# Layer 2's bias rows of a pair of heads placed side by side and fetched in one transfer

## The reference

```python
sim = jnp.einsum('bhid,bjd->bhij', q, k)          # 2 sequences, 16 heads, one shared k and v
sim = sim + jnp.concatenate([null_col, attn_bias], axis=-1)   # attn_bias: fside, (16, 1024, 1024)
sim = jnp.where(causal_mask, neg, sim)
sim = jnp.where(mask_p[:, None, None, :], sim, neg)
attn = jax.nn.softmax(sim, axis=-1)
out = jnp.einsum('bhij,bjd->bhid', attn, v)
```

## Time and profile before

| | |
|---|---|
| median of 3 runs | 2331.18 us (2331.05 to 2338.11) |
| the profiled execution, its own time | 2349.09 us |
| its span, first to last instruction | 2347.2 us |
| what lies around the span | 1.9 us |
| TensorE busy in the span | 85% |
| VectorE, ScalarE, GpSimd busy | 71%, 57%, 45% |
| mean granted TensorE clock | 0.928 |
| first to last `add_bias` of layer 1 / 2 / 3 | 450.5 / 480.9 / 437.6 us |

### The profile page before, as it was taken

One profiled execution on the slowest core, in us unless ns is written; L12 is line 12 of the kernel. 1 busy time (PEld: TensorE's weight loads), 2 busy tenths in 40 slices (PEclk: granted clock), 3 DMA queues, 4 the chain that ended last, 5 costly groups with the idle time before them and its releaser, 6 DMA issues. The chain is left out here.

```text
span 2347.2 us, 46857 instructions
## 1 busy us (share of the span) xinstructions
PE 2003.9 (85%) x11738; PEld 1429.2 (61%) x11738; DVE 1674.6 (71%) x4082; ACT 1338.9 (57%) x2900; POOL 1066.4 (45%) x1286
## 2 busy tenths in 40 slices
PE   5996496899999999389889999995595999999988
PEld 4885363666666667376556666665463666666657
DVE  5777766777887775558667877756665887888855
ACT  2222564677776664147557766642464777777753
POOL 1342113566765652006456666622112666666632
PEclk8998597899999999699889999998697999999999
DMA  4530246333333333386677777741246334333332
GB/s 119 157 127 17 85 170 246 113 109 108 108 109 108 108 104 113 102 299 191 205 226 229 235 233 231 231 157 34 92 171 235 100 108 123 119 118 107 115 121 87
DMA packets 222215, 338.76 MB, mean 144 GB/s; under 512 B 27446, under 2 KB 104380, under 8 KB 222044
## 3 DMA queue, kind: packets, MB, share of 16 engines
q1 hardware_dynamic: 222044, 336.86, 45.6%
HBM read 250.63 MB, written 102.91 MB: 151 GB/s over the span
## 5 line engine op out<-in xcount | busy, mean ns | idle before, releaser
L1486 POOL TENSOR_SCALAR at_row<-at_row,at_inv 128x129 f32<-128x129 f32 (+7 forms) x384 | 720.2, 1876 | 364.1 <-DVE at_inv L1647 357.3
L1694 ACT ACTIVATE at_row<-at_row,at_nmax 128x129 f32<-128x129 f32 (+7 forms) x768 | 595.3, 775 | 239.8 <-DVE at_nmax L1666 238.1
L1666 DVE CUSTOM_DVE_ANT_0 at_row<-at_s,bias,at_row 128x128 f32<-128x128 f32 (+7 forms) x768 | 618.1, 810 | 67.7 <-PE at_s L1594 39.6
L1606 PE MATMUL at_t<-ident,at_row 128*128 128x128 f32 x3456 | 549.5, 283 | 53.9 <-ACT at_pt L1687 33.9
L1606 PEld LDWEIGHTS at_t<-ident,at_row 128*128 128x128 f32 x3456 | 397.3, 143 | 259.1 <-issue 182.4
L1593 PE MATMUL at_s<-k_hh,q_hl 128*128 128x512 f32 (+3 forms) x1152 | 464.6, 403 | 48.2 <-SPq L1552 26.0
L1622 PE MATMUL at_o<-at_pt,v 128*64 128x512 f32 (+3 forms) x2304 | 443.4, 507 | 6.0 <-ACT at_pt L1687 2.5
L1501 DVE COPY at_pt<-at_t 128x128 f32<-128x128 f32 (+3 forms) x576 | 278.1, 483 | 204.6 <-PE at_t L1606 186.0
L1594 PE MATMUL at_s<-k_lp,q_h 65*128 65x512 f32 (+3 forms) x1152 | 393.7, 354 | 0.0
L1687 ACT ACTIVATE at_pt<-at_t 128x512 f32<-128x512 f32 (+2 forms) x576 | 307.3, 534 | 141.5 <-PE at_t L1606 136.3
L1593 PEld LDWEIGHTS at_s<-k_hh,q_hl 128*128 128x128 f32 x1152 | 226.5, 197 | 82.4 <-DVE at_nmax L1666 28.5
(11 more groups left out here) (225 smaller groups left out, 2813.9 us busy)
## 6 DMA issues: line engine op xcount, KB each, us to landing
q_hl<-q_dram SPq DMA_DIRECT2D x192, 256.0 KB, 4.3
bias<-bands_dram SPq DMA_DIRECT2D x64, 512.0 KB, 5.7
q_dram<-pj_qh SPq DMA_DIRECT2D x96, 256.0 KB, 2.7
q_dram<-pj_ql SPq DMA_DIRECT2D x96, 256.0 KB, 2.7
q_h<-q_dram SPq DMA_DIRECT2D x96, 256.0 KB, 5.0
o_dram<-at_o_sb SPq DMA_DIRECT2D x96, 256.0 KB, 4.5
o_in<-o_dram SPq DMA_DIRECT2D x10, 2048.0 KB, 8.5
bands_dram<-brow_dram SPq DMA_DIRECT2D x2, 8192.0 KB, 32.1
```

The costliest lines, as they stand in the source:

```text
L1486: return eng.tensor_scalar(cells, cells, inv[:, i:i + 1], None, ALU.mult)
L1606: last = eng.transpose(t_ps[m % NTR][:, c * P:(c + 1) * P], row[:, u % RING, here:here + P], t["ident"][:])
L1666: eng.tensor_tensor_reduce(out=row[:, u % RING, ZERO:ZERO + width], in0=s_ps[u % 2][:, 0:width], in1=bt[:, lo:lo + width], scale=-1.0, sca ...
L1694: eng.activation(cells, cells, ACT.Exp, scale=-1.0, bias=nmax[:, i:i + 1], accum_out=rsum[:, i:i + 1]).then_inc(s["exp"], 1)
```

## The change

Both units of a pair of heads get their bias rows in one place of twice the width, one unit's rows behind the other's in each partition. One transfer fetches the left part for both heads and one fetches both diagonal blocks, each with two runs for each partition instead of one. There are 8 semaphores for pairs instead of 16 for units, VectorE waits only ahead of the even unit, and the first seven pairs, as before the first fourteen units, are fetched in `project`.

```diff
-HEAD_SLOTS, BIAS_IN_FLIGHT, ROWS_FIRST = 4, 16, 14
+HEAD_SLOTS, PAIRS_IN_FLIGHT, PAIRS_FIRST = 4, 8, 7
...
-    widths = [((u // 2) % NT + 1) * P for u in range(4 * NT)]
+    widths = [2 * (k % NT + 1) * P for k in range(2 * NT)]
...
-        last.append(max(before + [u - BIAS_IN_FLIGHT]))
+        last.append(max(before + [k - PAIRS_IN_FLIGHT]))
...
-        if tile:
-            eng.dma_start(t["bias"][:, BIAS_AT[n]:BIAS_AT[n] + width - P],
-                          bias[one, tile * P:(tile + 1) * P, 0:width - P].rearrange("o p c -> p (o c)")).then_inc(sem, 16)
-        eng.dma_start(t["bias"][:, BIAS_AT[n] + width - P:BIAS_AT[n] + width],
-                      t["corners"][one, :, width - P:width].rearrange("o p c -> p (o c)")).then_inc(sem, 16)
+    tile = n % NT
+    width = (tile + 1) * P
+    two = bass.ds(head, 2)
+    out = t["bias"][:, PAIR_AT[n]:PAIR_AT[n] + 2 * width].rearrange("p (s c) -> p s c", s=2)
+    if tile:
+        eng.dma_start(out[:, :, 0:width - P], bias[two, tile * P:(tile + 1) * P, 0:width - P].rearrange("s p c -> p s c")
+                      ).then_inc(sem, 16)
+    eng.dma_start(out[:, :, width - P:width], t["corners"][two, :, width - P:width].rearrange("s p c -> p s c")).then_inc(sem, 16)
...
-                    place.wait(eng, "biased", BIAS_AFTER[n] + 1)
-                    p, tile, side, width = unit(n)
-                    load_bias(eng, t, bias, s[f"bias{n % NBIAS}"], n, place.turn * 2 * HP + (2 * p + side))
+                    place.wait(eng, "biased", 2 * PAIR_AFTER[n] + 2)
+                    load_bias(eng, t, bias, s[f"bias{n % NBIAS}"], n, place.turn * 2 * HP + 2 * (n // NT))
...
-                    for n in range(U):
-                        if n % GU == 0:
-                            queries(place, ready, n // GU)
-                        row_bias(place, ready, n)
+                    for n in range(U // 2):
+                        if n % (GU // 2) == 0:
+                            queries(place, ready, n // (GU // 2))
+                        pair_bias(place, ready, n)
...
-                    lo = (2 * p + side + 1) * S - width if toeplitz else BIAS_AT[u % U]
-                    if not toeplitz:
-                        turn.wait_loads(eng, f"bias{slot}", row_loads(u) * U // NBIAS, row_loads(u) * (u // NBIAS + 1))
-                    elif tile == 0:
+                    lo = (2 * p + side + 1) * S - width if toeplitz else PAIR_AT[u % U // 2] + side * width
+                    if not toeplitz and side == 0:
+                        turn.wait_loads(eng, f"bias{slot}", pair_loads(slot) * (U // 2 // NBIAS),
+                                        pair_loads(slot) * (u // 2 // NBIAS + 1))
+                    elif toeplitz and tile == 0:
```

More of the change, by code:

```diff
@@ L45, in bias_places, with pair_loads @@
     last = []
-    for u, width in enumerate(widths):
-        before = [n for n in range(u - len(widths), u)
-                  if places[n] < places[u] + width and places[u] < places[n] + widths[n]]
-        last.append(max(before + [u - BIAS_IN_FLIGHT]))
+    for k, width in enumerate(widths):
+        before = [n for n in range(k - len(widths), k)
+                  if places[n] < places[k] + width and places[k] < places[n] + widths[n]]
+        last.append(max(before + [k - PAIRS_IN_FLIGHT]))
     return places, last
-BIAS_AT, BIAS_AFTER = bias_places()
-def row_loads(n):
-    return 16 if (n // 2) % NT == 0 else 32
+PAIR_AT, PAIR_AFTER = bias_places()
+def pair_loads(k):
+    return 16 if k % NT == 0 else 32
 SERIAL = count()
@@ L966, in project @@
     LAST = N + 12
-    FIRST = HEAD_SLOTS if bias is None else ROWS_FIRST
+    FIRST = HEAD_SLOTS if bias is None else PAIRS_FIRST
     names = ["dve", "var", "std", "xn", "xtr", "xt_hi", "xt_lo", "main", "sq", "ss", "norm", "inv", "inv_t",
@@ L1051, in first_bias @@
                     for n in range(FIRST):
-                        load_bias(eng, t, bias, s["first"], n, n if bias is None else n % 2)
+                        load_bias(eng, t, bias, s["first"], n, n if bias is None else 0)
                 if bias is not None:
@@ L1070, in _ @@
                     eng.wait_ge(s[f"store{n}"], 32 * NCH * NPAIR // NST)
-                eng.wait_ge(s["first"], 96 + (16 * FIRST if bias is None else sum(row_loads(n) for n in range(FIRST))))
+                eng.wait_ge(s["first"], 96 + (16 * FIRST if bias is None else sum(pair_loads(n) for n in range(FIRST))))
             @block.tensor
@@ L1403, in load_bias @@
 def load_bias(eng, t, bias, sem, n, head):
-    one = bass.ds(head, 1)
     if bias is None:
[L1407 to L1410, removed]
-        if tile:
-            eng.dma_start(t["bias"][:, BIAS_AT[n]:BIAS_AT[n] + width - P],
-                          bias[one, tile * P:(tile + 1) * P, 0:width - P].rearrange("o p c -> p (o c)")).then_inc(sem, 16)
-        eng.dma_start(t["bias"][:, BIAS_AT[n] + width - P:BIAS_AT[n] + width],
-                      t["corners"][one, :, width - P:width].rearrange("o p c -> p (o c)")).then_inc(sem, 16)
+        eng.dma_start(t["bias"][:, n * S:(n + 1) * S], t["bands"][bass.ds(head, 1), :, :].rearrange("o p c -> p (o c)")
+                      ).then_inc(sem, 16)
+        return
+    tile = n % NT
[4 more added lines that the diff above has]
+        eng.dma_start(out[:, :, 0:width - P], bias[two, tile * P:(tile + 1) * P, 0:width - P].rearrange("s p c -> p s c")
+                      ).then_inc(sem, 16)
+    eng.dma_start(out[:, :, width - P:width], t["corners"][two, :, width - P:width].rearrange("s p c -> p s c")).then_inc(sem, 16)
 def load_outputs(eng, t, sem, c):
@@ L1438, in attend @@
     toeplitz = bias is None
-    NBIAS = HEAD_SLOTS if toeplitz else BIAS_IN_FLIGHT
-    n_bias = HP * 2 if toeplitz else U
+    NBIAS = HEAD_SLOTS if toeplitz else PAIRS_IN_FLIGHT
+    n_bias = HP * 2 if toeplitz else U // 2
     pieces, starts = [], []
@@ L1447, in attend @@
     NPC = len(pieces)
-    assert NPC % 6 == 0 and U % NBIAS == 0 and U % RING == 0 and NGRP % 2 == 0
+    assert NPC % 6 == 0 and n_bias % NBIAS == 0 and U % RING == 0 and NGRP % 2 == 0
     def first(u):
@@ L1463, in slot_loads @@
     def slot_loads(n):
-        return 16 if toeplitz else row_loads(n)
+        return 16 if toeplitz else pair_loads(n)
     def unit(u):
@@ L1528, in head_bias, with pair_bias @@
                     load_bias(eng, t, None, s[f"bias{n % NBIAS}"], n, place.turn * 2 * HP + n)
-                def row_bias(place, ready, n):
-                    if ready and n < ROWS_FIRST:
+                def pair_bias(place, ready, n):
+                    if ready and n < PAIRS_FIRST:
                         return
-                    place.wait(eng, "biased", BIAS_AFTER[n] + 1)
-                    p, tile, side, width = unit(n)
-                    load_bias(eng, t, bias, s[f"bias{n % NBIAS}"], n, place.turn * 2 * HP + (2 * p + side))
+                    place.wait(eng, "biased", 2 * PAIR_AFTER[n] + 2)
+                    load_bias(eng, t, bias, s[f"bias{n % NBIAS}"], n, place.turn * 2 * HP + 2 * (n // NT))
                 def loads(place, ready):
@@ L1552, in _ @@
                     eng.sem_inc(s[f"q{g}"], 48)
-                for n in range(HEAD_SLOTS if toeplitz else ROWS_FIRST):
+                for n in range(HEAD_SLOTS if toeplitz else PAIRS_FIRST):
                     eng.sem_inc(s[f"bias{n}"], slot_loads(n))
@@ L1658, in add_bias @@
                     turn.wait(eng, "qk", u + 1)
-                    slot = (2 * p + side if toeplitz else u) % NBIAS
-                    lo = (2 * p + side + 1) * S - width if toeplitz else BIAS_AT[u % U]
-                    if not toeplitz:
-                        turn.wait_loads(eng, f"bias{slot}", row_loads(u) * U // NBIAS, row_loads(u) * (u // NBIAS + 1))
-                    elif tile == 0:
+                    slot = (2 * p + side if toeplitz else u // 2) % NBIAS
+                    lo = (2 * p + side + 1) * S - width if toeplitz else PAIR_AT[u % U // 2] + side * width
[3 more added lines that the diff above has]
+                    elif toeplitz and tile == 0:
                         turn.wait_loads(eng, f"bias{slot}", 16, 16 * (u // U + 1))
```

## The result

The changed kernel takes 2321.4 us (median of 14 runs, 2318.38 to 2329.07), the kernel before 2335.69 us beside it (14 runs, 2331.05 to 2347.21). The ratio is 0.9937, 95% interval [0.9923, 0.9951], so the change is worth some 14.7 us (the medians are 14.3 apart). The forecast had 2314 us from 2331.18, a gain of 17.4.

The account below looks back on a forecast made before the run. SyncE's number of issues at turn starts was taken to bound layer 2's attention; -13.8 - 4 - 4 = -21.8 us profiled, four fifths of it -17.4, gave 2314 us from 2331.18, range 2299 to 2330.

Parts of the forecast that it names:

- What bounds the kernel: Layer 2's attention: some 43 us of waits caused by transfers, layer 3 the floor; turn starts limited by SyncE's issues, not bytes.
- The start of a turn, -13.8: Units 0 to 8, turns 1 to 7: fewer issues and earlier release cut 17.3 us of excess to 3.5.
- The two signs that the prediction named as fatal: Layer 2: a turn-start landing over 6 us after issue (B or D), or DMA share times stage over 351 us (D).
- The half microsecond of stall that it left: Start of each of seven turns: 0.5 us of stall left, as pair 4's margin is only 0.7 us.
- What follows, -4: Units 8 to 24: half of 8.8 us of pipeline refill and lower TensorE clock goes, between 0 and -8.8.
- VectorE's code, -4: Jumps in turns 1 and 2: both fetch again, but a shorter backlog saves 4 of 18.3 us.
- Waits added, 0: Pairs 7 and 15 in SyncE's queue: their new waits for units 7 and 23 cost nothing.
- Four fifths: Whole kernel: plain runs gain four fifths of the profiled -21.8 us, so -17.4, as they may stall less.
- B: Turn starts: data come no earlier because two-run issues take SyncE longer; 2324 to 2331 us, say 2327; chance 0.17.
- D: Left parts' transfers: two runs of a partition, 4 MiB apart, slow each other; 2410 us if twice as long; chance 0.05.
- E: Jumps of turns 5 and 6 begin to stall by the code's place, spending the gain; 2332 us; chance 0.07.
- C: VectorE's code stalls in turns 1 and 2 go as well, 17.5 us instead of 4; 2301 us; chance 0.13.

Follow-up runs that it names:

- run 3: Changed kernel plus two idle semaphore increments ahead of layer 2's attention in VectorE's code; 2302.33 us beside 2340.7 of before, ratio 0.9836.
- run 1: Changed kernel with one transfer per head again (four issues for a pair instead of two), new places and early release kept; 2331.96 us beside 2340.7, ratio 0.9960.
- run 2: Changed kernel with pairs 0 to 2 waiting for unit 30 of the turn before, not 29; 2334.88 us beside 2340.7 of before, ratio 0.9968.
- run 6: Changed kernel with left parts after the layer's first turn cut to 128 columns, same number of issues, other results; one execution, 2314.12 us.
- run 5: Kernel before plus two idle semaphore increments at the head of VectorE's layer 2 stream; 2321.69 us beside 2338.39, ratio 0.9925.
- run 7: Changed kernel with 32 idle increments ahead of layer 1's VectorE loop, none in layer 2, 50 ahead of layer 3's; 2298.32 us beside 2338.39, ratio 0.9830.
- run 9: Run 7 once more, on one chip with a repeat of run 3; 2297.98 us beside 2337.44 of before, ratio 0.9830.
- run 4: Changed kernel with twenty idle increments ahead of layer 2's VectorE code, which move layer 3's loop too; one execution, 2310.87 us.

## Why the prediction was right or wrong

**What bounds the kernel**: right in the main. Layer 3 was the floor, to the microsecond once everything is removed (run 3: 437.8 against 437.0), and run 1 keeps the issues and keeps most of the stall before unit 8. But "the number of issues, not the bytes" was too sharp: with half the issues and the old release (run 2) the DMA share is 0.97 to 1.03 in these windows and 13.9 of the 17.3 us stay.

**The start of a turn, -13.8**: measured -14.4. Two of its inputs were off and cancelled. The issues were 0.56 us apart instead of 0.62, so pair 4 was out 4.5 us after unit 0 and not 5.4; it took 7.2 us to land in turn 1 and not 5.3. The landing grew mostly by the backlog ahead of it, since parts of the same 128 KB landed in 3.7 us (median) in run 6; a landing read in a window with a DMA share of 0.75 does not hold for one at 0.99. The two signs that the prediction named as fatal, a landing over 6 us and a DMA share times stage over 351 (0.78 × 461.8 = 360), both came true without their consequence: they were set too tight. The half microsecond of stall that it left in each turn is there: 0.52, 0.68 and 0.58 us ahead of unit 8 in turns 1 to 3. The prediction put both edits into one line of times and did not say what either gives alone. For unit 8's bias both were needed; for the stage as a whole each alone gave more than half (runs 1 and 2).

**What follows, -4**: measured -9.4, more than the 8.8 us that were there; half was too low. Most of it hangs on VectorE's waits just behind unit 8, which went with the queries' lateness: they are gone in runs 1 and 2 as well, where unit 8's bias is still late. Runs 5 and 3, which have no code stall, show 6.2 us of it between them: units 8 to 16 go from 117.2 to 111.0 us and units 16 to 24 stay at 80.1.

**VectorE's code, -4**: this is the step that failed. Its first half held: a removed wait removes no instruction, the loop's place stayed, both jumps fetched again twice. Its second half, that "the backlog is shorter" since SyncE is ahead of its work, had the sign wrong: the stalls grew by 4.7 us. An issuer that is ahead has more transfers in flight, and a fetch of code waits behind them: at the two branches the last of them landed 6.9 and 9.5 us later, where before it was 4.1 and 4.4, and run 6 shows the same fetches at less than half with fewer bytes. Runs 1 and 2, with half of the change each, had sums of branch-to-head and head-to-copy of 26.2 and 24.1 us over the two jumps, where before had 22.1 and the changed kernel 26.8. Each is one execution, so the order of the two is not settled.

**Waits added, 0**: right. No row of the waits names `bias` or `q_h` any more, and the half microsecond ahead of unit 8 is pair 4's, which this term does not cover.

**Four fifths**: the three terms came to -19.1 in the profile for a forecast -21.8; the step to plain runs took off a fifth. Measured, plain runs gained 14.7. Each stage against 480.9 and each ratio on 2335.69, the stage gains 3.7, 4.3, 4.4, 4.8 and 5.3 us more than the plain runs in run 1, run 2, the changed kernel, run 3 and run 5: nearly the same amount for gains from 7 to 38 us, though each of these gains has an interval of 3 to 7 us either way. So it looks like no factor but an offset: the profiled execution of before was itself some 4 us slow in this stage, as its 2349 us had hinted. This is argued from the numbers, not shown by a second profile of before. Layer 1's gain in runs 7 and 9 does not fit this and is the part left open.

**The rivals.** B (0.17, the data come no earlier) is refuted by the windows of units 0 to 8, though its condition, a later landing, was met. D (0.05, two runs for each partition slow each other) is refuted: summed over layer 2's stage the packets of the data queue took 360.8 us of 16 engines, and 349.4 in the stage of before, 3% more, but in run 1, where each transfer has one run again, they took 359.3; the corners' packets of 512 bytes and the longest of 3584 have the same medians as before, 27 and 140 ns. The Trainium skill, "DMA: Bandwidth & Descriptors", Latency and other measured facts, halves the rate for partitions 4 MiB apart; here, with partitions 4 KiB apart and two runs 4 MiB apart within each, nothing of that is seen. E did not occur in the changed kernel, but run 4 made it occur in layer 3, at 2.3 to 2.5 us a turn for one fetch at light load. C (0.13) needed the place to move by two instructions: it did not happen, and run 3 shows what it gives, a ratio of 0.984 where C's 2301 us are 0.987.

The place can be counted. If VectorE's code comes in pieces of 256 instructions and two are held, a loop of 304 instructions fits in two pieces or needs three, by where it starts. Counted from the program, layer 2's first loop head is the last instruction of its piece: one fetch for it and one right behind for the next, which are the two serial stalls. Two instructions on, it is the second of the next piece, and three pieces become two. The Trainium skill, "Advanced Engine Details and Errata", ISA Cache, gives just these numbers; the traces agree in all that was tried: layer 1's loops, which by the count need three pieces but do not start at an edge, stall once for 2.8 to 3.0 us; layer 3's fit, and cease to fit with 20 more (run 4); run 7's shifts, chosen by the count, stall nowhere.

The traces can be asked for the size without the page. By the instructions that they record on VectorE, the six loops have 301, 301, 304, 304, 301 and 301 instructions, and in the changed kernel the later five heads lie 526, 1309, 1838, 2771 and 3297 instructions behind the first. Suppose that a loop stalls when it touches more than two pieces. With the place of the first head in its piece left free, 256 is the only size from 40 to 700 that gives all 24 outcomes of the changed kernel and runs 3, 4 and 7. Three held pieces of 128 would give them too, so the number held is what these runs leave open. That layer 2's first head ends its piece can be seen: between the two stalls VectorE's queue runs one instruction, the loop's first, at 1127.8, and the next starts at 1134.0.

## What to carry to other kernels

When an issuing queue is the limit, count both what it issues and when it may begin. Here each alone gave more than half of the gain, but the first transfers that a turn needs came in time only with both, since halving the issues handed the limit to the bytes. Judge an experiment by the whole stage: a window that ends at one late unit shows only what that unit waited for. Before tuning transfers around a hardware loop, read the time from the loop's branch to its first instruction on every engine: a stall of 3 to 14 us in some turns and none in others is the code's place, and a few idle instructions ahead of the loop test it in one run. Do not expect such a stall to shrink when transfers are issued sooner.

## What the runs showed of the hardware

A fetch of VectorE's code at a jump took 2.8 to 3.6 us where the stage's DMA share was 0.38 (layer 1, and layer 3 in run 4), 2.5 to 3.1 at 0.65 and 4.9 to 7.5 at about 0.9 (the kernel before, the changed one, runs 1 and 2): it queues behind data. The first stall of the changed kernel in slices of two microseconds (windows):

```profile
1126.00:1128.00 2.00, 0.00 (x0) 0.00 (x0) 0.00 (x0) 0.00 (x0) 0.00 (x0) 0.74 0.83 195
1128.00:1130.00 2.00, 0.00 (x0) 0.00 (x0) 0.00 (x0) 0.00 (x0) 0.00 (x0) 0.50 1.05 235
...
1132.00:1134.00 2.00, 0.00 (x0) 0.00 (x0) 0.00 (x0) 0.00 (x0) 0.00 (x0) 0.50 1.06 357
...
1136.00:1138.00 2.00, 2.00 (x7) 0.76 (x6) 2.00 (x5) 1.67 (x3) 1.81 (x1) 0.50 0.09 31
```

All compute engines stand for VectorE's code while the DMA engines work at full share (0.83 to 1.06); then, as VectorE goes on, they run dry, since SyncE had waited for it and issued nothing from 1129.6 to 1138.2 us. TensorE's granted clock goes from 1.0 to 0.5 (1.2 GHz) in the stall and is still there as the work resumes, which is the second cost of a stall: 0.79 and 0.80 over these windows of units 8 to 16.

An issue with two runs in each partition took SyncE 0.37 us, with one run 0.33, and the next followed after 0.56 instead of 0.51 to 0.55 us: two issues made one save nearly half of the time.
